# Four negated row maxima per step in one group of 32-row products, in an attention and feed-forward kernel

## What is computed

```python
def _L0_attn_ref(x, gamma, beta, w_qkv):
    B, N, E, H = (2, 512, 256, 16)
    b, n, e = x.shape
    h, d = (H, E // H)
    mu = jnp.mean(x, axis=-1, keepdims=True)
    var = jnp.mean(jnp.square(x - mu), axis=-1, keepdims=True)
    xn = (x - mu) * jax.lax.rsqrt(var + LN_EPS) * gamma + beta
    qkv = jnp.einsum('bne,fe->bnf', xn, w_qkv)
    q, k, v = jnp.split(qkv, 3, axis=-1)
    q = to_heads(q) * d ** (-0.5)
    ...
    sim = jnp.einsum('bhqd,bhkd->bhqk', q, k)
    sim = jnp.where(causal_mask, neg, sim)
    attn = jax.nn.softmax(sim, axis=-1)
    out = jnp.einsum('bhqk,bhkd->bhqd', attn, v)
    return out.transpose(0, 2, 1, 3).reshape(b, n, h * d)
...
x = _layernorm(x + _L0_attn_ref(x, gamma, beta, w_qkv), axis=-1)
x = _layernorm(x + _L0_ffn_ref(x, w1_w, ...), axis=-1)
```

## Time and profile before

| | us |
|---|---|
| median of 3 runs | 2339.94 |
| lowest and highest run | 2337.88, 2340.47 |
| the profiled execution | 2337.86 |
| its span (first to last instruction) | 2336.3 |
| mean granted TensorE clock | 0.994 of full |

### The profile page before, as it was taken

The page is one execution under the profiler, slowest core; times in us unless marked ns, Lnnn a source line. Parts: engine busy times, 40 slices in busy tenths (PEclk is TensorE's granted clock), DMA queues, the critical chain, the costliest instruction groups (busy, mean ns, idle before and its releaser), DMA issues. The chain is left out here.

```text
span 2336.3 us, 40349 instructions
## 1 busy us (share of the span) xinstructions
PE 2300.7 (98%) x15394; PEld 1407.0 (60%) x15394; DVE 1739.6 (74%) x3755; ACT 1607.0 (69%) x3164; POOL 207.0 (9%) x268
## 2 busy tenths in 40 slices
PE   8999999999999999999999999999899999999998
PEld 4555554555555555555555555554588888888886
DVE  8899997988889887888888889995335444554543
ACT  4677787888989887888978889999523323332332
POOL 3211100011000101000010211001000000000000
PEclk9999999999999999999999999999899999999999
DMA  3110001100000200000021000205400000000000
GB/s 100 29 27 19 1 19 39 37 19 20 19 19 1 57 23 16 19 19 19 1 55 28 22 8 19 73 1 199 147 1 10 1 10 10 10 1 10 10 1 19
DMA packets 38997, 66.49 MB, mean 28 GB/s; under 512 B 9361, under 2 KB 19473, under 8 KB 37393
## 3 DMA queue, kind: packets, MB, share of 16 engines
q1 hardware_dynamic: 35136, 52.35, 8.2%
q0 software_dynamic: 3664, 11.53, 1.6%
HBM read 28.20 MB, written 4.19 MB: 14 GB/s over the span
## 5 line engine op out<-in xcount | busy, mean ns | idle before, releaser
L679 ACT ACTIVATE PR<-bank 128x512 f32<-128x512 f32 (+3 forms) x2304 | 1108.2, 571 | 80.3 <-PE bank L972 78.1
L768 DVE TENSOR_REDUCE pm<-bank 128x1 f32<-128x512 f32 x1476 | 947.5, 682 | 165.2 <-PE bank L947 148.0
L986 PE MATMUL bank<-PR,V 128*17 128x512 f32 (+3 forms) x4608 | 559.7, 562 | 1.9 <-ACT PR L679 1.2
L1340 PE MATMUL bank<-e_hid,e_h_sb 128*128 128x512 f32 x2048 | 477.2, 395 | 0.0
L967 PE MATMUL bank<-MR,ones 64*128 64x512 f32 (+3 forms) x2304 | 457.5, 386 | 1.7 <-DVE pm L768 0.7
L1340 PEld LDWEIGHTS bank<-e_hid,e_h_sb 128*128 128x128 f32 x2048 | 385.5, 188 | 90.3
L1158 ACT ACTIVATE e_tmp<-bank,e_s_sb 128x512 f32<-128x512 f32 x128 | 88.2, 689 | 341.2 <-PE bank L1340 340.9
L967 PEld LDWEIGHTS bank<-MR,ones 64*128 64x128 f32 x2304 | 233.0, 186 | 70.8 <-ACT PR L679 29.3
L771 DVE CUSTOM_DVE_ANT_0 bank<-bank,below 128x256 f32<-128x256 f32 (+3 forms) x512 | 236.2, 519 | 21.3 <-PE bank L947 20.1
L1281 DVE CAST e_hid<-e_tmp 128x512 fp32r<-128x512 f32 x128 | 54.4, 425 | 258.0 <-ACT e_tmp L1158 258.0
L947 PE MATMUL bank<-KA,QX 64*128 64x512 f32 (+2 forms) x992 | 241.3, 441 | 1.2
(11 more groups left out here) (121 smaller groups left out, 1744.8 us busy)
## 6 DMA issues: line engine op xcount, KB each, us to landing
xnT<-in_h_dram SPq DMA_DIRECT2D x8, 1024.0 KB, 5.3
e_h_sb<-in_h_dram POOLq DMA_DIRECT2D x2, 4096.0 KB, 19.9
KA<-qk_hi SPq DMA_DIRECT2D x88, 64.0 KB, 2.3
KA<-qk_lo SPq DMA_DIRECT2D x88, 64.0 KB, 2.2
QX<-qk_hi SPq DMA_DIRECT2D x80, 64.0 KB, 2.3
QX<-qk_lo SPq DMA_DIRECT2D x80, 64.0 KB, 2.3
xres<-in_x_dram SPq DMA_DIRECT2D x8, 512.0 KB, 8.0
out_dram<-e_y SPq DMA_DIRECT2D x7, 512.0 KB, 2.9
```

Source lines behind the costliest of these rows:

```text
L679: act.activation(PR[:, s % NPB, h, off:QB], ring_bank("score", s, h)[:, off:QB], ACT.Exp).then_inc(exp_done, 1)
L768: dve.reduce_max(pm[:, B % 2, i, a, p, 1 + c:2 + c], bank[:, :], AX.X).then_inc(mx_done, 1)
L986: last = pe.matmul(ACC[32 * h:32 * h + VW, off:QB], V[:, v_tile(B, t), GH * (B // NJ % 2) + h, :], PR[:, s % NPB, h, off:QB], start=(t == ...
L1340: last = pe.matmul(RING[(4 + n) % NR][:, :], w[:, c, P * o:P * (o + 1)], hid[:, (T + layer) % 2, part, c, :], start=(c == 0 and part == 0) ...
```

## The change

The negated maxima of the four heads get 32 rows each instead of sharing halves of 64. In `mneg` the columns of head h = 2p + a move from 64a + 2p to 64a + 32p (two columns each, high part and rest), and so do the rows of `MR` after the transposition. `ones` has one version instead of one per p, with ones in rows 0, 1, 32, 33, 64, 65, 96 and 97. `score(s, 0)` now issues the products of maxima for all four heads, each on its own 32 rows and with its own bank, and `score(s, 1)` issues none; the products of keys and queries stay as they are, 64 rows each. The banks that `take_banks` gives to each use do not change, nor does `PLAN.ops`.

```diff
--- before.py
+++ after.py
@@ -324,7 +324,7 @@
         KA = sb("KA", [P, NKA, 2, QB], fp32r)
         QA = sb("QA", [P, NQA, 2, QB], fp32r)
         MR = sb("MR", [P, NM, QB], fp32r)
-        ones = sb("ones", [P, 2, P], fp32r)
+        ones = sb("ones", [P, P], fp32r)
         V = sb("V", [P, NV * TI, VH, VW])
         PR = sb("PR", [P, NPB, GH, QB])
         wg = sb("wg", [P, 2, EC, 2 * GE])
@@ -784,12 +784,12 @@
                 dve.wait_ge(rowmax_done, B + 1)
                 if B >= 1:
                     dve.wait_ge(mt_ready, B)
-                column = mneg[:, :, :].rearrange("q i (a y p s) -> q i a y p s", a=2, p=2, s=2)
-                dve.tensor_scalar(column[:, :, :, 0, :, 0], rowmax[:, B % NX, :, :, :], -1.0, None, ALU.mult)\
+                column = mneg[:, :, :].rearrange("q i (a p y s) -> q i a p y s", a=2, p=2, s=2)
+                dve.tensor_scalar(column[:, :, :, :, 0, 0], rowmax[:, B % NX, :, :, :], -1.0, None, ALU.mult)\
                    .then_inc(mneg_hi, 1)
                 dve.wait_ge(mneg_hi, B + 1)
-                dve.scalar_tensor_tensor(out=column[:, :, :, 0, :, 1], in0=rowmax[:, B % NX, :, :, :], scalar=-1.0,
-                                         in1=column[:, :, :, 0, :, 0].bitcast(fp32), op0=ALU.mult, op1=ALU.subtract)\
+                dve.scalar_tensor_tensor(out=column[:, :, :, :, 0, 1], in0=rowmax[:, B % NX, :, :, :], scalar=-1.0,
+                                         in1=column[:, :, :, :, 0, 0].bitcast(fp32), op0=ALU.mult, op1=ALU.subtract)\
                    .then_inc(mneg_done, 1)
 
             def invert_sums(B):
@@ -817,13 +817,10 @@
             def constants():
                 dve.memset(ACC[:, :], 0.0).then_inc(acc_zero, 1)
                 dve.wait_ge(consts, 2)
-                pairs = ident[:, :].rearrange("q (a y p s) -> q p y a s", a=2, p=2, s=2)
-                for p in range(2):
-                    dve.tensor_reduce(picked[:, p:p + 1], pairs[:, p, 0, :, :], axis=AX.XY, op=ALU.max)\
-                       .then_inc(picked_done, 1)
-                for p in range(2):
-                    dve.wait_ge(picked_done, p + 1)
-                    dve.tensor_copy(ones[:, p, :], picked[:, p:p + 1].broadcast_to([P, P])).then_inc(ones_done, 1)
+                heads = ident[:, :].rearrange("q (h y s) -> q h y s", h=GH, s=2)
+                dve.tensor_reduce(picked[:, 0:1], heads[:, :, 0, :], axis=AX.XY, op=ALU.max).then_inc(picked_done, 1)
+                dve.wait_ge(picked_done, 1)
+                dve.tensor_copy(ones[:, :], picked[:, 0:1].broadcast_to([P, P])).then_inc(ones_done, 1)
                 by_16 = ident[:, :].rearrange("q (a y d) -> q y a d", y=2, d=D)
                 by_32 = ident[:, :].rearrange("q (a y d) -> q y a d", y=2, d=2 * D)
                 for side, lows in ((0, by_16), (1, by_32)):
@@ -961,11 +958,11 @@
                 off = offset(B, t)
                 if t == 0 and p == 0:
                     pe.wait_ge(mrow_done, B + 1)
-                for a in range(2):
-                    h = 2 * p + a
+                for h in range(GH if p == 0 else 0):
+                    own = slice(HALF * (h % 2) + HALF // 2 * (h // 2), HALF * (h % 2) + HALF // 2 * (h // 2 + 1))
                     ring_free("score", s, h)
-                    pe.matmul(ring_bank("score", s, h)[:, off:QB], ones[rows(a), p, :],
-                              MR[rows(a), B % NM, off:QB], start=True, stop=False)
+                    pe.matmul(ring_bank("score", s, h)[:, off:QB], ones[own, :], MR[own, B % NM, off:QB],
+                              start=True, stop=False)
                 keys = slice(P * (t % TI), P * (t % TI + 1))
                 for a in range(2):
                     h = 2 * p + a
@@ -996,7 +993,7 @@
                 last.then_inc(at_ready, 1)
 
             pe.wait_ge(consts, 2)
-            pe.wait_ge(ones_done, 2)
+            pe.wait_ge(ones_done, 1)
             pe.wait_ge(acc_zero, 1)
             for op in PLAN.ops:
                 if op[0] == "norm":
```

## The result

The changed kernel takes 2497.74 us (median of 4 runs, 2496.58 to 2504.82) against 2339.47 us: 1.0685 times as long, 95% interval 1.0672 to 1.0698. It is slower by 158 us. The prediction said 2555 and 219 us more; the direction and the range (2420 to 2625) hold, and the size is 57 us too high.

What follows compares the result with a forecast made beforehand. TensorE was taken to bound the attention, with VectorE and ScalarE close behind. Shape changes and bank waits added 135, 50 and 34 us over three groups of steps, 219 on 2337.9, said as 2555 us; range 2420 to 2625.

Steps and rivals of the forecast that it cites:

- The bound, and one step: In the attention TensorE is busy 1514 of 1520 us, VectorE and ScalarE 86% each; a plain step takes 2.60 us.
- Shape: Two more changes of the array's shape per step, around the four maxima products: 0.19 us a step, 94 us.
- Rival B: No cost for 64 to 32 rows, but the wait for banks holds: 84 us more, 2422 us; chance 0.13.
- Four side by side: The four 32-row products of maxima run side by side as pairs do, saving one 0.23 us pair per step.
- rival D: The 32-row products run only two at a time: 0.23 us more per full step, 2665 us; chance 0.06.
- The bank wait: Four banks, not two, must be free before line 972's first pair: rounds of 3.14 us against 2.60.
- the first term of the sum: 270 steps of 2.30 to 2.70 us each get 0.50 us longer: 135 us.
- The second term: 128 steps of 2.70 to 3.15 us each get 0.39 us longer: 50 us.
- the third: 177 other steps, narrow or with projections and transpositions, each get 0.19 us longer: 34 us.
- The signs: Profile after: maxima products 0.34 us behind the unit pair, ScalarE's waits over 150 us, busy shares about 77%, steps 3.05 to 3.15.
- A: TensorE's extra work counts, the wait for banks doesn't: 94 us more, 2432 us; chance 0.10.
- C: No shape cost and banks free in time: 0.23 us goes from each full step, 2220 us; chance 0.07.

Runs made afterwards that it cites:

- replanned kernel: Changed kernel with banks dealt out by a plan that takes a step's four banks at once and counts the shape changes: 2449.69 us, ratio 1.0474.
- short exponentials: Changed kernel with exponentials of heads 2 and 3 over half the columns on full-width steps: 2461.88 us; same cut in the kernel before: 2339.68 us.
- 32 rows in the old places: Kernel before with each head's maxima on 32 rows of their own, products still two ahead of each key-query pair: 2685.36 us, ratio 1.1477.

## Why the prediction came out as it did

**The bound, and one step.** Right as far as it was tried: with ScalarE 200 us less busy the kernel before took the same time. No run took work from VectorE.

**Shape.** Right in kind, and near in size. A pair between two changes of 64 and 32 rows takes 0.43 in place of 0.23. That is the rule of the Trainium skill, "TensorEngine Tiling (Array Packing)", Key Properties, that a change of mode drains the engine, and the trace agrees. The steps that I had let come out even, those with value products, a projection or a transposition right ahead of the quad, are 79, and they did: -2 us together in the replanned kernel. The other 496 gained 0.22 each there, 110 us, for a forecast of 0.19 and 94: 0.20 between full-width quads (417 steps), 0.31 on the rest. Two things are in the surplus. The 0.19 was worked out for full width and used for narrow steps as well, though a narrow pass that goes saves less than 0.23. And banks are still waited for: the time by which a quad's fourth load starts behind its first comes to 37 us in the replanned kernel, against 68 in the changed one. Some of these waits the kernel before had in other places, so what shape costs by itself lies near the 94 but is not measured. Rival B, no shape cost, is out.

**Four side by side.** Right; rival D is out. The quad takes 0.44 from start to start, as long as a 32-row *pair* between the same neighbours, 0.43. By the 3.07-fold speed for four row tiles in the Trainium skill, "TensorE: Matmul & The Clock Gate", Part 3, it would be 0.07 longer (an estimate from that figure); the trace shows 0.01.

**The bank wait.** The round was right to the hundredth: 3.14 forecast, 3.14 found. Its frequency was the step that failed: "Where a reduction frees the last bank the round comes out about alike". It does not: such rounds come out at 2.78, those of the last exponential at 3.14. By the bank plan and the trace of before, the latest of the four banks came from a reduction in 185 and from the last exponential in 82 of the 270 ordinary steps. Before the change that reduction ended 2.48 after line 972's first pair (median), next to the exponential's 2.55; after it the two are at 2.29 and 2.66. In the changed kernel the second reduction after the scores ends 2.30 after line 969's first pair (696.29 from 693.99), not 2.6 as in the earlier trace rows (631.1 from 628.51). The reduction in the earlier trace rows is a late one, so this is more than the 0.19 between the medians. Two things made the difference, and both could be read off. The unit pair now follows the first pair by 0.58 (694.57 from 693.99), where it followed by 0.70 (629.21 from 628.51), since the second pair of maxima no longer stands between. And VectorE had a queue of reductions; with a step 0.18 longer it has none and starts 0.43 after the unit pair (695.00), not 0.61 (629.82). I had moved the exponentials and the reductions by the same 0.10 and forgotten that the change also takes something out from between. So a wait of 0.36 falls on some 61 to 66 steps instead of all 270, and the first term of the sum is 72 us instead of 135. The second term, 39.7 for 50, is too large as well, and the third, 44.9 for 34, too small. In that third group the 58 steps that already changed shape ahead of the quad gained 1 us together and the other 119 gained 0.37 each: the sum gave 0.19 to all 177, against the prediction's own count of 80 steps that come out even. By luck the 11 us too little there took back a part of the 74 too much in the other two terms.

**The signs.** ScalarE's waits (227 us) and the 0.44 behind the quad came as said. The quad starts 0.43 behind the unit pair and not the 0.34 of that list; the 0.34 left out the emptying of the array, which the prediction's own sum had. VectorE and ScalarE fell to 82% and 79%, not to 77%, and steps of 3.05 to 3.15 are 66 of the 270.

**The clock.** I expected it to stay. It did in the middle, but not at the start, where TensorE waits more, nor around 443 us. The changed kernel, 40 to 110 and 430 to 470 us:

```profile
40.00:110.00 70.00, 66.38 (x369) 32.64 (x368) 53.46 (x136) 33.16 (x73) 17.48 (x20) 0.83 0.12 30
...
430.00:470.00 40.00, 36.51 (x232) 16.43 (x231) 26.62 (x74) 24.77 (x52) 5.11 (x6) 0.87 0.24 58
```

and the kernel before, 40 to 110 us:

```profile
40.00:110.00 70.00, 68.23 (x450) 38.07 (x449) 62.06 (x158) 40.07 (x86) 18.62 (x21) 0.95 0.11 27
```

A mean of 0.83 between the two levels (2.4 and 1.2 GHz) is 24 us at 1.2 GHz in the 70, against 7 us before; the 0.87 is 10 us more. These 27 us at half speed cost 14 at most. That would fall mostly on steps at the start, and it is an estimate: no run changed the clock alone.

**Rivals A and C.** A (shape alone, 2432) is what the short exponentials and the new plan come near, with 2462 and 2450: the bank wait was real in the kernel as it is, and a quarter to a third of the loss went with it (36 and 48 of 158 us, the latter by the plan alone and with up to 9 us of clock in it). Since neither kernel is rid of all its waits, the wait's whole share may be larger. C, faster, had no part that held.

None of the kernels here beats the one before.

## What to carry to other kernels

Count the shape of the array as a resource: a product that packs more heads into finer rows saves a pass of 0.23 us here and pays two changes at 0.20 each, so by these figures, an estimate, it pays only where its neighbours have the same shape or where at least two passes go (0.46 against 0.40), which no run here tried. Products grouped together ask for all their buffers at once; look up in the plan of buffers who gives each back, and plan the buffers anew with the order. When a step is lengthened, work out anew each releaser's distance from its own trigger, since a queue on another engine may dissolve and what stood between two instructions may be gone.

## What the runs showed of the hardware

Changing between 64 and 32 rows costs what 128 to 64 does: about 0.10 us until the next load starts (0.43 less 0.34 with 32 rows in the old places, 0.09), and 0.10 to 0.11 for a load of 128 columns that starts with its own product instead of one pair ahead. Four 32-row products of 512 columns take as long as two, 0.44 against 0.43. A load that waits for a bank starts 0.05 after the exponential (687.22 to 687.28) or the reduction (696.29 to 696.34) has ended. The view of waits books the emptying of the array as a wait for another engine: 408 times 0.28 us for "ACT PR L679", most of which was none.
